# Attention probabilities: split in query order and turned by DMA, with value products two tiles behind

## What is computed

```
q = rope(rms_norm(x @ Wq.T));  k = rope(rms_norm(kv @ Wk.T));  v = kv @ Wv.T
probs = softmax(q @ k.T * SCALE)          # k, v repeated for the 4 heads of a key head
x = x + (probs @ v) @ Wo.T
```

## Time and profile before

| | |
|---|---|
| median of 3 runs | 2138.7 us (2136.3 to 2139.9) |
| the profiled execution | 2131.0 us, span 2129.2 us |
| mean granted TensorE clock | 0.908 |
| TensorE busy | 1805.2 us, 85% of the span |
| VectorE busy | 1453.1 us, 68% |
| ScalarE busy | 1074.8 us, 50% |
| GpSimd busy | 1080.8 us, 51% |
| DMA | 202.6 MB moved, mean 95 GB/s |

### The profile page before, as it was taken

One profiled execution on the slowest core, in us unless ns is written; L12 is line 12 of the kernel. 1 busy time (PEld: TensorE's weight loads), 2 busy tenths in 40 slices (PEclk: granted clock), 3 DMA queues, 4 the chain that ended last, 5 costly groups with the idle time before them and its releaser, 6 DMA issues. The chain is left out here.

```text
span 2129.2 us, 44379 instructions
## 1 busy us (share of the span) xinstructions
PE 1805.2 (85%) x14711; PEld 1352.4 (64%) x14711; DVE 1453.1 (68%) x3940; ACT 1074.8 (50%) x2650; POOL 1080.8 (51%) x1641
## 2 busy tenths in 40 slices
PE   3447999999999999999999999757888887378997
PEld 3425788777777877877877787543544444136884
DVE  7746887877778778778868877646445554456656
ACT  2414766666666666766767766520222222054443
POOL 4413786676667659657756865100345544154110
PEclk8657999999999999999999999956989998676998
DMA  6671022112202202201220203332367766420100
GB/s 264 245 306 71 2 82 82 35 50 82 82 3 82 82 3 82 82 28 57 82 83 2 82 12 101 108 140 81 108 192 215 212 203 180 139 56 9 41 15 24
DMA packets 74760, 202.58 MB, mean 95 GB/s; under 512 B 9945, under 2 KB 40770, under 8 KB 71170
## 3 DMA queue, kind: packets, MB, share of 16 engines
q1 hardware_dynamic: 61346, 163.70, 22.8%
q0 software_dynamic: 9984, 30.42, 4.4%
q10 hardware_dynamic: 3168, 5.24, 0.7%
HBM read 161.67 MB, written 37.66 MB: 94 GB/s over the span
## 5 line engine op out<-in xcount | busy, mean ns | idle before, releaser
L857 DVE TENSOR_TENSOR att_pT<-att_pT 128x512 bf16<-128x512 f32 (+1 forms) x512 | 321.9, 651 | 198.4 <-ACT att_pT L754 195.7
L616 PE MATMUL att_out<-att_V,att_pT 128*128 128x128 bf16 x5760 | 385.9, 219 | 10.0 <-DVE att_pT L857 8.3
L754 ACT ACTIVATE att_pT<-att_pT 128x512 bf16<-128x512 f32 (+1 forms) x512 | 278.3, 572 | 201.4 <-PE att_pT L604 201.4
L616 PEld LDWEIGHTS att_out<-att_V,att_pT 128*128 128x128 bf16 x5760 | 350.2, 98 | 36.7 <-DVE att_pT L857 19.6
L760 ACT ACTIVATE att_prob<-att_scores,att_negmax 128x512 f32<-128x512 f32 (+1 forms) x512 | 329.5, 653 | 15.8 <-DVE att_negmax L846 14.6
L595 PE MATMUL att_scores<-att_K,att_Q 128*128 128x512 bf16 (+1 forms) x1536 | 331.0, 366 | 0.0
L844 DVE TENSOR_REDUCE att_mx<-att_scores 128x1 f32<-128x512 f32 (+1 forms) x512 | 292.2, 631 | 4.6 <-PE att_scores L595 4.5
L604 PE MATMUL att_pT<-att_ident,att_prob 128*128 128x128 f32 x1920 | 278.2, 276 | 17.4 <-issue 17.4
L595 PEld LDWEIGHTS att_scores<-att_K,att_Q 128*128 128x128 bf16 x1536 | 153.0, 100 | 149.0 <-issue 11.0
L555 PE MATMUL att_aux<-att_wkv,att_kvT 128*128 128x256 bf16 x1440 | 188.1, 282 | 42.4 <-DMA att_kvT<-kv_s 21.1
L604 PEld LDWEIGHTS att_pT<-att_ident,att_prob 128*128 128x128 f32 x1920 | 211.5, 142 | 19.1 <-issue 18.2
(11 more groups left out here) (299 smaller groups left out, 3286.2 us busy)
## 6 DMA issues: line engine op xcount, KB each, us to landing
moe_wa<-in_wa_l SPq DMA_DIRECT2D x80, 480.0 KB
att_kvT<-kv_s SPq DMA_DIRECT2D x16, 1920.0 KB
att_tab<-tab_s SPq DMA_DIRECT2D x16, 960.0 KB
att_wq<-wq_s SPq DMA_DIRECT2D x16, 512.0 KB
att_wo<-wo_s SPq DMA_DIRECT2D x16, 512.0 KB
kv_s<-prep_kvhl SPq DMA_DIRECT2D x4, 1920.0 KB
prep_kv<-in_ctx_l SPq DMA_DIRECT2D x4, 1664.0 KB, 7.6
moe_y<-y_s SPq DMA_DIRECT2D x8, 768.0 KB, 4.6
```

The lines of the kernel that those rows point to most:

```text
L616: last = nc.tensor.matmul(out_ps[:, i % 2, :], pT[:, i % 2, a, k, :], V[:, par, k, w, :], start=(k, a, w) == (0, 0, 0), stop=(k, a) == (KT ...
L754: nc.scalar.activation(pT[:, i % 2, 0, 4 * j:4 * j + m, :], pT_ps[j % 2][:, 0:m, :], ACT.Copy).then_inc(s["pt_hi"], 1)
L857: nc.vector.tensor_tensor(pT[:, i % 2, 1, 4 * j:4 * j + m, :], pT_ps[j % 2][:, 0:m, :], pT[:, i % 2, 0, 4 * j:4 * j + m, :], ALU.subtract) ...
```

## The change

In words:

- ScalarE copies the exponentials, still with queries in the partitions, as bf16 (`probs_high`), VectorE subtracts to get the low half (`probs_low`), both from SBUF, in two spans of 1024 and 833 columns instead of four banks. Maxima and exponentials go by the same two spans.
- SyncE turns each half with one DMA transpose per tile, 128x1920 bf16 from SBUF to SBUF (`turn`): 256 transposes in all. TensorE's float32 transposes are gone.
- TensorE's value products are of the tile two before, and the tail has five slots instead of three.
- `aux` is two banks, used in turn; the output has a bank per tile parity.
- SyncE's program goes slot by slot. Both turns of the tile before stand at the head of each slot; the loads of the next group stand behind them in slot 0, its wo in slot 4.
- `SLOTS` has another order: Q 0 and Q 1 in slot 0, ahead of all KV; AT and WO of the group before, and the KT, later. `POOL_ORDER` follows it.
- The buffer of the window gather shares the memory of `tab`.

```diff
+SPANS = [(k, min(1024, NK - k)) for k in range(0, NK, 1024)]
...
 SLOTS = [
+    ([], [("Q", 0)], [("Q", 1)]),
     ([], [("KV", 0)], [("KV", 1)]),
-    ([("AT-", 1)], [("KV", 2)], [("WO-", 1)]),
-    ([], [("Q", 0)], [("KV", 3)]),
-    ([], [("Q", 1)], [("KV", 4)]),
-    ([("KT", 0)], [("KV", 5)], [("KV", 6)]),
-    ([("AT", 0)], [("KV", 7)], [("QT", 0)]),
-    ([("KT", 1)], [("WO", 0)], [("QT", 1)]),
-    ([("KT", 2)], [("KT", 3)], []),
+    ([], [("KV", 2)], [("AT-", 1)]),
+    ([], [("KV", 3)], [("KV", 4)]),
+    ([], [("WO-", 1)], [("KV", 5)]),
+    ([], [("KV", 6)], [("KV", 7), ("KT", 0)]),
+    ([], [("QT", 0), ("KT", 1)], [("AT", 0), ("QT", 1)]),
+    ([], [("KT", 2)], [("WO", 0), ("KT", 3)]),
 ]
-FIRST_GROUP = [("KV", 0), ("KV", 1), ("KV", 2), ("Q", 0), ("KV", 3), ("Q", 1), ("KV", 4), ("KV", 5), ("KV", 6),
+TAIL = 5
+FIRST_GROUP = [("Q", 0), ("Q", 1), ("KV", 0), ("KV", 1), ("KV", 2), ("KV", 3), ("KV", 4), ("KV", 5), ("KV", 6),
                ("KV", 7), ("QT", 0), ("QT", 1), ("KT", 0), ("KT", 1), ("KT", 2), ("KT", 3)]
-POOL_ORDER = [x for x in FIRST_GROUP if x[0] in ("KV", "Q")]
+POOL_ORDER = [x for slot in SLOTS for place in slot for x in place if x[0] in ("KV", "Q")]
...
         rsum, rinv = sc.sb("rsum", [P, 4]), sc.sb("rinv", [P, 4])
...
+        phl = sc.sb("phl", [P, 2, 2, KP], BF16)
...
+        windows = tab[:, :, :, :, :].rearrange("p u a k f -> p (u a k f)")[:, 0:2 * WIN * ROW].rearrange("p (u n) -> p u n", u=2)
...
-        pT_ps = [sc.ps(f"pT{i}", [P, 4, P]) for i in range(2)]
-        out_ps = sc.ps("out", [P, 2, HD])
-        aux = sc.ps("aux", [P, 512])
+        out_ps = [sc.ps(f"out{i}", [P, 512]) for i in range(2)]
+        aux_ps = [sc.ps(f"aux{i}", [P, 512]) for i in range(2)]
...
-                def load_group(n, par, b, h):
+                def load_first(n, par, b, h):
                     if not isinstance(n, int) or n >= 2:
-
-                        sp.wait_ge(s["kp_done"], nth("KV", PAIRS - 1, n - 2))
-                        sp.wait_ge(s["qp_done"], nth("Q", 1, n - 2))
+                        keys, queries = nth("KV", PAIRS - 1, n - 2), nth("Q", 1, n - 2)
+                        sp.wait_ge(s["kp_done"], keys)
+                        sp.wait_ge(s["qp_done"], queries)
                     for dst, src in ((wkv[:, par, :, :, :].rearrange("p a c n -> p (a c n)"), t["wkv_s"][h]),
                                      (kvT[:, par, :, :, :].rearrange("p a c k -> p (a c k)"), t["kv_s"][b])):
                         sp.dma_start(dst, src).then_inc(load[par], 16)
                     sp.dma_start(wq[:, par, :, :, :].rearrange("p a c n -> p (a c n)"), t["wq_s"][h]).then_inc(wq_load[par], 16)
                     sp.dma_start(tab[:, par, :, :, :].rearrange("p a k f -> p (a k f)"), t["tab_s"][b]).then_inc(tab_load[par], 16)
...
+                def load_wo(n, par, h):
                     if not isinstance(n, int) or n >= 2:
                         sp.wait_ge(s["wo_done"], nth("WO", 1, n - 2))
                     sp.dma_start(wo[:, par, :, :, :].rearrange("p a h n -> p (a h n)"), t["wo_s"][h]).then_inc(wo_load[par], 16)
...
-                load_group(0, 0, 0, 0)
-                load_group(1, 1, 0, 1)
-                if groups > 2:
-                    with sp.Fori(1, groups // 2) as p:
-                        for u in range(2):
-                            load_group(2 * p + u, u, p // 2, 2 * (p % 2) + u)
+                def batch_head(g, u, ahead):
+                    n, par = g + ahead, (u + ahead) % 2
+                    if isinstance(n, int):
+                        return n, par, n // KVH, n % KVH
+                    half = (g - u + 2 * ((u + ahead) // 2)) // 2
+                    return n, par, half // 2, 2 * (half % 2) + par
+
+                def turn(tile, i, half, done, turned):
+                    sp.wait_ge(s[done], NS * (tile + 1))
+                    sp.sem_inc(s["turning"], 1)
+                    sp.dma_start_transpose(pT[:, i % 2, half, :, :], phl[:, i % 2, half, :]).then_inc(turned[i % 2], 16)
+
+                def slot(i, g, u, first, prep, last):
+                    if not (first and i == 0) and not (last and i > 0):
+                        turn(TILES * g + i - 1, (i - 1) % TILES, 0, "p_hi", turned_hi)
+                        turn(TILES * g + i - 1, (i - 1) % TILES, 1, "p_lo", turned_lo)
+                    if i == 0 and prep and not first:
+                        load_first(*batch_head(g, u, 1))
+                    if i == 4 and prep and not first:
+                        n, par, _, h = batch_head(g, u, 1)
+                        load_wo(n, par, h)
+
+                sp.wait_ge(s["pad"], 4)
+                load_first(0, 0, 0, 0)
+                for dst, src in ((kw, "kw_l"), (qw, "qw_l"), (ident, "ident_l")):
+                    sp.dma_start(dst[:, :], t[src]).then_inc(s["const"], 16)
+                sp.dma_start(segt_i[:, :], t["segt_l"]).then_inc(s["seg_in"], 16)
+                load_wo(0, 0, 0)
+                load_first(1, 1, 0, 1)
+                load_wo(1, 1, 1)
+                each_group(sp, lambda g, u, first, prep: [slot(i, g, u, first, prep, False) for i in range(TILES)],
+                           lambda g: [slot(i, g, 0, False, False, True) for i in range(TAIL)])
...
-                    if before:
-                        bk, bn, bg = before.pop()
+                    if len(before) == 2:
+                        bk, bn, bg = before.pop(0)
                         wait(pe, s[FREE[bk]], nth(bk, bn, bg))
                     before.append((kind, n, gt))
+                    aux = aux_ps[turn_of[0] % 2]
+                    turn_of[0] += 1
...
-                        wait(pe, s["exp_done"], NB * (tile - 1) + k + 1)
+                        wait(pe, s["exp_done"], NS * (tile - 1) + k // 2 + 1)
...
                     if j == 0:
-                        wait(pe, s["o_done"], tile)
-                    pe.wait_ge(s["pt_lo"], NB * tile + j + 1)
+                        if i == 0:
+                            pe.wait_ge(s["v_lo"], nth("KV", PAIRS - 1, g))
+                        wait(pe, s["o_done"], tile - 1)
+                        done = 16 * (TILES // 2 * g + i // 2 + 1)
+                        pe.wait_ge(turned_hi[i % 2], done)
+                        pe.wait_ge(turned_lo[i % 2], done)
                     for m in range(quad(j)):
                         k = 4 * j + m
                         for a, w in ((0, 0), (0, 1), (1, 0)):
-                            last = nc.tensor.matmul(out_ps[:, i % 2, :], pT[:, i % 2, a, k, :], V[:, par, k, w, :],
+                            last = nc.tensor.matmul(out_ps[i % 2][:, 0:HD], pT[:, i % 2, a, k, :], V[:, par, k, w, :],
                                                     start=(k, a, w) == (0, 0, 0), stop=(k, a) == (KT - 1, 1))
...
-                    old = not (first and i == 0) and not (last and i > 0)
-                    tile, oi = TILES * g + i - 1, (i - 1) % TILES
-                    og, opar = (g, u) if i else (g - 1, 1 - u)
-                    if old:
-                        turn_probs(tile, oi, 0)
-                        turn_probs(tile, oi, 1)
+                    old = not (first and i < 2) and not (last and i > 1)
+                    tile, oi = TILES * g + i - 2, (i - 2) % TILES
+                    og, opar = (g, u) if i >= 2 else (g - 1, 1 - u)
                     if not last:
                         form_scores(g, u, i)
                     for x_ in ahead:
                         task(*x_, g, u)
                     if old:
                         apply_values(tile, oi, 0, og, opar)
-                        turn_probs(tile, oi, 2)
                         apply_values(tile, oi, 1, og, opar)
-                        turn_probs(tile, oi, 3)
...
-                def probs_high(tile, i, j):
-                    act.wait_ge(s["pt_done"], NB * tile + j + 1)
-                    m = quad(j)
-                    nc.scalar.activation(pT[:, i % 2, 0, 4 * j:4 * j + m, :], pT_ps[j % 2][:, 0:m, :], ACT.Copy).then_inc(s["pt_hi"], 1)
+                def probs_high(tile, i, g, k):
+                    lo, n = SPANS[k]
+                    act.wait_ge(s["exp_done"], NS * tile + k + 1)
+                    if k == 0:
+                        wait(act, turned_hi[i % 2], 16 * (TILES // 2 * g + i // 2))
+                    nc.scalar.activation(phl[:, i % 2, 0, lo:lo + n], prob[:, i % 2, lo:lo + n], ACT.Copy).then_inc(s["p_hi"], 1)
 
...
                     if k == 0:
                         act.wait_ge(s["negmax_ready"], tile + 1)
-                    lo, n = BANKS[k]
+                        wait(act, s["p_lo"], NS * (tile - 1))
+                    lo, n = SPANS[k]
                     nc.scalar.activation(prob[:, i % 2, lo:lo + n], scores[:, lo:lo + n], ACT.Exp, bias=negmax[:, i % 4:i % 4 + 1],
...
-                    if not (first and i < 2) and not (last and i > 1):
-                        output(tile - 2, (i - 2) % TILES)
```

(43 more changed lines are left out.)

58 lines of the change are left out of this document (21 added, 37 removed).

## The result

The changed kernel took 2432.0 us (median of 4 runs, 2425.0 to 2476.1) where the kernel before took 2139.3: 1.133 times as long by the means, with a 95% interval of 1.122 to 1.144. That ratio leaves out the execution of 2476.1 us, which fell into a slower state of the chip. The forecast was 2225 us, slower, from 2105 to 2480. So the sign and the range held, and the size did not: +293 us where the sum gave +87. The profiled execution took 2433.9 us (span 2432.1), 303 more than the one of before, and 294 of these lie inside the attention stage, which ended at 1670.8 us instead of 1376.6.

What follows compares the result with a forecast made beforehand. TensorE bounded the attention stage before; late loads and GpSimd's rope chain would then set the period at 82 us against 74.7. Periods +103, group 0 -7, last group -9: +87, so 2225 us, range 2105 to 2480.

Steps and rivals of the forecast that it cites:

- The loads' place: SyncE, slot 0: loads stand behind both turns, so TensorE waits for wq, 12 us of each period, in 14 periods.
- T+21: Arrival of tab, the last load, releasing GpSimd's rope chain; T is the start of scores in slot 0.
- third rival: Attention slots bound by the DMA transposes: at 6 us each, period 108 us, time about 2670 us; chance 0.20.
- The stage's own sum: Attention stage: start at 183.8 us, group 0 of 67, 14 periods of 82, last group of 64.
- Period = 21 + 52.1 + 8.4 + 0.6 = 82: Each group: arrival of tab, GpSimd's rope chain, its contention with VectorE and the last turn, against 74.7 us before.
- The last group ... 64 against 73, -9: Group without projections: 8 slots bounded by scores, maximum, exponential or two transposes (6 us), and a drain of about 17.
- I take 3 us: One 480 KB SBUF-to-SBUF transpose on SyncE's queue, issues included; bounds 1.1 and 8.2 us.
- rival 2: Contention of 16 us and transposes of 4.4: tab at T+24, period 93, about 2385 us; within the main case's 0.62.
- Contention by the whole-instruction lock: VectorE's subtractions stop GpSimd fully: 16 us per group, period 90; the sum used 0.6 us each, 8.4 per group.
- the forecast's sum (195): TensorE loses 13.0 us of transposes per group: 195 us gained over 15 groups if nothing else moved.

Runs made afterwards that it cites:

- Experiment 4: Changed kernel with VectorE's subtraction cut to 64 columns of each span, the low half otherwise left out: 2226.5 us, ratio 1.045 to the kernel before.
- Experiment 9: Changed kernel with GpSimd's eight gathers of window rows held back until the last value product of the attention stage: 2457.2 us.
- experiment 3: Changed kernel with the loads issued ahead of the two turns of slot 0, still for the next group: 2289.5 us, ratio 1.076 to the kernel before.
- experiment 1: Changed kernel with the loads issued two groups ahead instead of one: 2189.0 us, ratio 1.028 to the kernel before.

## Why the prediction was right and wrong

**What held.** TensorE lost its transposes and was not the bound any more. The loads' place did decide: TensorE waited 13.7 to 14.8 us for wq where I said 12 at the least, and it did so in 14 periods, as forecast (the fifteenth wait of the row, 23.3 us, stands ahead of group 0). GpSimd's chain came next and set the period. It began at T+21.9 in the group shown, against T+21, but what released it was not the arrival of `tab`, as I had it: the loads' traffic was all but over at 645 us, T+19.8 (DMA share 0.06 from 645 to 646), and GpSimd waited on for ScalarE's copy of the first query block, which stands behind the wait on wq. The number is close in part by luck. The slot was not bound by the transposes, so the third rival was rightly the smaller case.

**What failed.** The stage's own sum was 183.8 + 67 + 14 x 82 + 64 = 1463 us, the stage ended at 1671. The 208 us between are 14 x (94.5 - 82) = 175 for the periods and 33 for the last group. Group 0 took 250.84 - 178.02 = 72.8 us against 67, and began 5.8 us earlier than in the kernel before (178.0 against 183.8); the two cancel. Its chain began at 184.48, 6.5 us in where I said 6, and took 65.7 us where I said 60.5: the same term was too small there. Another 8 us lie in the later stages, which I did not study.

*The step "Period = 21 + 52.1 + 8.4 + 0.6 = 82".* This is the step that failed. In the group shown it reads 21.9 + 69.7 + 5.5 = 97.1, and in the mean of the 14 periods 22.4 + 69.6 + 2.5 = 94.5. The middle term, the chain with its contention, was 60.5 and became 69.6: 9 of the 12.5 us by which a period was too short. Of the 9 us, contention took 2 (10.4 for 8.4, inside its bounds of 2 to 16). Six are a wait that I had put at nothing, GpSimd's for VectorE's squares of the queries: 85.3 us over 15 groups. The list of waits of before had its like, 6.8 us at the longest for the squares of the keys, in a chain that then had 192.8 / 15 = 12.9 us to spare per group (its wait for ScalarE's copy); I took the chain's length from a stretch of it without such a wait. These six are read from the trace; no run took this wait alone out of the changed kernel. About one microsecond more is spread over the chain. The last term was 0.6 and became 5.5 to 5.8 in five of the 14 periods, those that end at a boundary of the hardware loop, and 0.7 to 0.9 in the others. Behind that pause of some 5 us the scores that restart TensorE took 4.4 us where 2.3 to 2.5 is usual, at a granted clock of 0.50 in the stretch 722 to 727, the lower of its two levels (1.2 and 2.4 GHz), and the next loads were issued 10.4 us behind their start instead of 8.7. Experiment 4 shows that these terms are coupled: take the subtraction away, 10.2 us of contention, and the period falls to (1301.17 - 332.21) / 12 = 80.7 us between load issues, by 14.

*The step "The last group ... 64 against 73, -9".* It had the terms for maxima and transposes right in kind, but took 3 us per transpose with nothing beside them. They took 4.3 us at the median, and 7.0 beside the window gathers, whose traffic the trace of before already showed in that very stretch. Experiment 9 separates the two: 22 us from the gathers, 11 from the turns' latency and the slot's own loop.

*The step "I take 3 us" for a transpose.* Over the whole stage 4.1 us at the least, 4.4 at the median, 11.5 at the most; its issue took 1.3 us on SyncE at the least, 1.6 at the median and 5.9 at the most. The median lies inside the bounds. Its main cost was the one that I had priced under the loads: it makes SyncE a queue in which they stand behind VectorE's work, 143 us in experiment 3. Time to landing is not the time that the queue needs: in the last group of experiment 9 the 18 transposes, with next to nothing beside them, kept the 16 DMA engines busy for 77.0% of 64 us, an estimate of 2.7 us each. Rival 3 priced the queue by the time to landing; at 4.4 us that would be 82 us of queue in a period, and in experiment 1 a period took (1342.95 - 250.91) / 14 = 78.0 us with every transpose in place. In rival 2 my working was off as well: a transpose of 4.4 us in place of 3 moves `tab` from T+21 to T+22.4, not to T+24. By the Trainium skill, page DMA: Bandwidth & Descriptors, section Latency and other measured facts, a DMA transpose moves 261 GB/s with a non-contiguous middle dimension, an estimate of 1.9 us for 480 KB. The runs show 4.4 us to landing (which holds the fixed parts of a transfer too), and the measurement decides.

*Contention by the whole-instruction lock.* The sum took half of an instruction each, the lock would have taken all of it: 16 us. The runs show 10.2 to 10.4 us per group with two SBUF operands, and nothing with one in PSUM (1078.9 us busy). The Trainium skill, page SBUF — State Buffer, section Who interferes with whom, says that a VectorE instruction with two SBUF inputs contends with a GpSimd instruction that reads SBUF, and that one with at most one, outside VectorE's two-port modes, does not. By that, the trace agrees about which operands matter. The lock for a whole instruction, which the prediction took from that section, is said there of the two-port modes; for two SBUF inputs it gives no size. The size measured lies between my half and the whole.

**Left open.** The wait of TensorE for the copies of turned queries (98.1 us over 15 groups, in slot 6) was not taken apart: ScalarE's copy of the last key block there waits for GpSimd's `kp`, and the reordered tasks stand behind it. It falls where GpSimd is already the bound, so it should cost little in the changed kernel; no run here shows that. Nor was a version tried with loads and transposes on different issuing engines.

## What to carry to other kernels

When a wait is put on an engine that only issues DMAs, everything behind it in its program waits too: list what stands there and when it is first needed, since the loads of the next group cost more here (243 us) than the transposes that left TensorE were worth by the forecast's sum (195). Moving work from a bound engine shows its gain only if the chain that comes second is priced with its waits, from the wait list and not only from its instructions' durations. And a DMA put on a critical loop must be priced with the DMA traffic that already runs in that stretch, whichever queue issues it.

## What the runs showed of the hardware that I had not expected

A DMA transpose of 128x1920 bf16 from SBUF to SBUF took 4.1 us at the least; behind loads on the same queue up to 13.4 us (experiment 1), and beside gathers issued by GpSimd, on another queue, 7.0 at the median. The count of packets rose from 74,760 to 574,427, of which 509,658 are under 512 bytes. From the changed kernel's view of the tile (duration of the issue on SyncE in ns, min/median/max, and time to landing):

```profile
L541 SPq DMA_TRANSPOSE att_pT<-att_phl x256: 1306/1604/5915, 186.6 to 1656.1; - x128
...
DMA to landing us min/median/max: 4.1/4.4/11.5
```

Contention between VectorE and GpSimd follows the place of one operand: the same subtraction, on the same shape, cost GpSimd 10.2 us per group with its input in SBUF and nothing measurable with it in PSUM. And TensorE came out of each 14 us wait at the lower of its two levels: 6 products of 512 columns took 2.74 us at 643.69, 0.46 each, at a granted clock of 0.50 from 643 to 646, where the next five, at 648.85, took 1.24, 0.25 each. The 14 waits were 13.7 to 14.8 us long, and the six products behind each took 2.72 to 2.74 us.
